# A six-layer model on one core: causal mask by matmuls, totals inverted in a compact form, matmuls in TensorE's gaps

## The reference

```python
x = x + 0.5 * L0_ffn(ln(x))     # gated feed-forward, hidden size 512, ternary weights
x = x + L0_attn(ln(x))          # linear attention: theta, phi, g
x = x + 0.5 * L0_ffn(ln(x))
x = x + 0.5 * L1_ffn(ln(x))     # 8 low-rank experts, 2 chosen for each sequence
x = x + L1_attn(ln(x))          # causal softmax attention, 16 heads of 8, rotary positions
x = x + 0.5 * L1_ffn(ln(x))
```

## Time and profile before

| | |
|---|---|
| median of three runs | 767.94 us (765.27 to 769.16) |
| profiled execution | 768.91 us, of which span 765.8 us |
| TensorE busy | 656.6 us (86%), granted clock 0.931 in the mean |
| VectorE, ScalarE, GpSimd busy | 524.9, 504.1, 311.3 us |
| GpSimd selects (L1264) | 128, 79.8 us |
| 128x256 reciprocals (L1091) | 15, 26.2 us |
| DMA | 18.2% of 16 engines' span |

### The profile page before, as it was taken

The page is one execution under the profiler, slowest core; times in us unless marked ns, Lnnn a source line. Parts: engine busy times, 40 slices in busy tenths (PEclk is TensorE's granted clock), DMA queues, the critical chain, the costliest instruction groups (busy, mean ns, idle before and its releaser), DMA issues.

```text
span 765.8 us, 13407 instructions
## 1 busy us (share of the span) xinstructions
PE 656.6 (86%) x4878; PEld 468.1 (61%) x4878; DVE 524.9 (69%) x1306; ACT 504.1 (66%) x830; POOL 311.3 (41%) x433
## 2 busy tenths in 40 slices
PE   2889989999999998999999897877778778888673
PEld 1667766787777787777787774544445445545442
DVE  3745465677657755677678659988799867879342
ACT  2867677977689858878778952365545666655541
POOL 2200121143423130225345467566747665446432
PEclk9989999999999999999999998699889998989785
DMA  9100000000110000000111123134444353431111
GB/s 296 42 1 1 0 1 1 0 1 2 42 41 1 0 1 1 1 0 1 42 42 42 42 114 113 51 118 144 136 138 136 132 192 118 144 126 58 56 57 29
DMA packets 47083, 47.21 MB, mean 62 GB/s; under 512 B 3240, under 2 KB 41128, under 8 KB 46760
## 3 DMA queue, kind: packets, MB, share of 16 engines
q1 hardware_dynamic: 47016, 46.33, 18.2%
HBM read 23.51 MB, written 22.54 MB: 60 GB/s over the span
## 4 chain that ended last, share of the span: by engine, by line
PE 50%; DVE 17%; ACT 12%; DMA 8%; issue 6%; SPq 4%; POOL 2%; POOLq 0%; DVEq 0%; ACTq 0%
PE PSA L769 15%; PE PSA L773 14%; DMA LC<-do 5%; DVE MX L1070 5%; ACT PSA L1122 3%; PE PSA L935 2%; SPq L1316 2%; PE PSA L786 2%; DVE LC L1091 2%; DVE G L993 2%; DMA QS<-dq 2%; PE PSA L882 2%; ACT G L1118 2%; PE PSA L875 2%; ACT ah L1129 1%
## 5 line engine op out<-in xcount | busy, mean ns | idle before, releaser
L1216 POOL TENSOR_TENSOR RS<-VE,MHALF 128x4 f32<-128x4 f32 x48 | 49.3, 1027 | 228.6 <-DVE VE L975 228.4
L769 PE MATMUL PSA<-ah,WH 128*128 128x512 f32 x320 | 131.8, 412 | 9.0 <-DVE al L998 4.8
L1070 DVE TENSOR_REDUCE MX<-PSA 128x6 f32<-128x768 f32 x128 | 117.2, 945 | 16.3 <-PE PSA L904 16.3
L773 PE MATMUL PSA<-al,WH 128*128 128x512 f32 x320 | 125.9, 393 | 0.0
L1122 ACT ACTIVATE PSA<-PSA,SC 128x512 f32<-128x512 f32 x128 | 84.7, 661 | 55.4 <-PE PSA L773 54.8
L1198 ACT ACTIVATE PB<-PSA 128x768 f32<-128x768 f32 x128 | 99.0, 818 | 16.1 <-PE PSA L922 15.9
L769 PE MATMUL PSA<-bh,WH 128*128 128x512 f32 x256 | 104.7, 409 | 4.8 <-DVE al L998 1.7
L773 PE MATMUL PSA<-bl,WH 128*128 128x512 f32 x256 | 100.2, 392 | 0.0
L1264 POOL TENSOR_SCALAR_AFFINE_SELECT PB<-PB 128x512 f32<-128x512 f32 x128 | 79.8, 635 | 45.2 <-ACT PB L1198 43.6
L998 DVE TENSOR_TENSOR al<-PSA,ah 128x512 fp32r<-128x512 f32 x64 | 44.2, 691 | 67.0 <-ACT ah L1129 67.0
L769 PEld LDWEIGHTS PSA<-ah,WH 128*128 128x128 f32 x320 | 60.5, 189 | 27.0 <-DVE al L998 7.1
(11 more groups left out here) (120 smaller groups left out, 1355.9 us busy)
## 6 DMA issues: line engine op xcount, KB each, us to landing
do<-OT SPq DMA_DIRECT2D x15, 512.0 KB, 4.7
KS<-dk SPq DMA_DIRECT2D x32, 192.0 KB
QS<-dq SPq DMA_DIRECT2D x32, 192.0 KB
dk<-CB SPq DMA_DIRECT2D x16, 192.0 KB, 2.3
dq<-CB SPq DMA_DIRECT2D x16, 192.0 KB, 2.5
X<-in_x SPq DMA_DIRECT2D x8, 256.0 KB, 6.9
dk<-CB SPq DMA_DIRECT2D x16, 128.0 KB, 1.9
dq<-CB SPq DMA_DIRECT2D x16, 128.0 KB, 1.9
```

The lines of the kernel that those rows point to most:

```text
L769: e.matmul(o, WH[:, col:col + 128], hi, start=first, stop=False)
L773: return e.matmul(o, WH[:, col:col + 128], low, start=False, stop=last)
L1070: e.tensor_reduce(MX[:, u % 2, :, :].rearrange("p t (l g) -> p l t g", l=2)[:, :, :, g], PSA[:, b:b + 2, 0:384].rearrange("p l (t k) -> p ...
L1216: e.tensor_tensor(RS[:, i, :], VE[:, i, :], MHALF[:, :], ALU.pow).then_inc(g_rs, 1)
```

## The change

1. `pass2`: `affine_select` on GpSimd goes. Four matmuls ahead of the scores add -1e30 where keys lie after the query, from the identity IM and a new constant ML (two more casts on GpSimd in `mark`, a masks input of 384 KB for 256). `weigh` waits for ScalarE's exp.
2. For units 0 to 13 the totals are inverted once for each head and query: `tot_in` loads one row of totals for each head as 128x32 (TOT), `inverse` inverts it on VectorE, `tot_out` writes it to DRAM, `vl_in` loads it to LC with a broadcast over the eight rows of a head. `norm_out` waits for the loads. Unit 14 keeps the load and reciprocal of before, the reciprocal placed up to 3 us earlier in the plan; unit 15 keeps `spread`. The layouts of DO, WO and SEL change to match.
3. `fill`: after `mark`, wherever the planned start of a TensorE step lies after the end of the one before, a step `keep` with up to 65% of the gap in 128x128 bf16 matmuls (identity times identity, 0.06 us each in the plan) goes in before it. It writes to the bank that is free first, which nobody reads.

```diff
-    "pass2": [("P", 0.18, 0.34), ("A", 0.69, 0.81), ("G", 0.59, 0.63)],
+    "pass2": [("P", 0.34, 0.5), ("A", 0.69, 0.81)],
+    "tot_in": [("S", 0.5, 0.5), ("D", 2.6)], "inverse": [("V", 0.28, 0.36)],
+    "tot_out": [("S", 0.5, 0.5), ("D", 2.6)], "vl_in": [("S", 1.12, 1.12), ("D", 3.7)], "recip": [("V", 1.66, 1.74)], "norm_out": [("G", 0.68, 0.72)],
+FILLED = 0.65
...
+            if eng == "P":
+                self.fill(s0)
+                self.idle_from = s0 + us
...
+    def fill(self, t):
+        free = {b: f for b, f in [*enumerate(self.bank), *self.sr.free.items()] if f}
+        if not free or not self.count.get("mark"):
+            return
+        b = min(free, key=lambda b: self.left(free[b]))
+        n = int((t - max(self.idle_from, self.left(free[b]) + 0.06) - 0.15) * FILLED / 0.06)
+        if n > 1:
...
+            self.steps.insert(-1, Step("keep", k, x=n, b=b, emptied=free[b]))
...
             yield from self.until(o.done - 0.5)
+            if u < NB - 2:
+                o = self.put("tot_in", u=u, src=o)
+                yield from self.until(o.done)
+                o = self.put("inverse", u=u, src=o)
+                yield from self.until(o.done - 0.2)
+                o = self.put("tot_out", u=u, src=o)
+                yield from self.until(o.done - 0.5)
             ld = self.put("vl_in", u=u, src=o, emptied=self.vcfree[u % 2])
             self.vcfree[u % 2] = None
-            yield from self.until(ld.done)
-            rc = self.put("recip", u=u, src=ld)
-            on = self.put("norm_out", u=u, src=rc)
+            yield from self.until(ld.done - 3.0 * (u == NB - 2))
+            if u == NB - 2:
+                ld = self.put("recip", u=u, src=ld)
+                yield from self.until(ld.done - 0.2)
+            on = self.put("norm_out", u=u, src=ld)
...
+                elif st.name == "keep":
+                    w.wait_ge(g_c, 4)
+                    emptied(w, st.emptied)
+                    for _ in range(st.x):
+                        e.matmul(PSA[:, b, 0:128], IDB[:, :], IDB[:, :], start=True, stop=True)
...
+                    for k in (1, 0):
+                        for h in range(2):
+                            e.matmul(PSA[:, b + h, 0:256].rearrange("p (t q) -> p t q", t=2)[:, :, 0:64 + 64 * k],
+                                     IM[64 * h:64 * h + 64, k, :], ML[64 * h:64 * h + 64, k, :, 0:64 + 64 * k],
+                                     start=(k == 1), stop=False, skip_group_check=True)
...
-                    w.wait_ge(g_sel, 8 * u + 2 * g + 2)
+                    w.wait_ge(a_prob, 8 * u + 2 * g + 2)
...
+                elif st.name == "inverse":
+                    w.wait_ge(s_tot[u % 2], 16 * (u // 2 + 1))
+                    e.reciprocal(TOT[:, u % 2, :], TOT[:, u % 2, :]).then_inc(v_inv, 1)
...
-                elif st.name == "pass2":
-                    w.wait_ge(a_prob, n + 1)
-                    e.affine_select(out=P, in_=P, compare_op=ALU.is_ge, fill=0.0, base=0,
-                                    pattern=[[0, 4], [1, 128]], channel_multiplier=-1).then_inc(g_sel, 1)
                 elif st.name == "norm_out":
-                    w.wait_ge(v_rc, st.src.n + 1)
+                    if st.src.name == "recip":
+                        w.wait_ge(v_rc, st.src.n + 1)
+                    else:
+                        w.wait_ge(s_vl[u % 2], 32 * (u // 2 + 1))
...
+                elif st.name == "tot_in":
+                    w.wait_ge(s_dv[u % 2], 16 * (u // 2 + 1))
+                    w.wait_ge(s_inv[u % 2], 16 * (u // 2))
+                    e.dma_start(TOT[:, u % 2, :], DO[u, 8].rearrange("v g (a b) -> (v g a) b", b=32)).then_inc(
+                        s_tot[u % 2], 16)
+                elif st.name == "tot_out":
+                    w.wait_ge(v_inv, st.src.n + 1)
+                    e.dma_start(DI[u].rearrange("v g (a b) -> (v g a) b", b=32), TOT[:, u % 2, :]).then_inc(
+                        s_inv[u % 2], 16)
...
+                        w.wait_ge(s_inv[u % 2], 16 * (u // 2 + 1))
+                        totals = DI[u:u + 1].rearrange("o v g t -> o (v g) t").to_broadcast([8, 16, S])
```

More of the change, by code:

```diff
@@ L141, in __init__ @@
         self.table = self.pe = ""
+        self.idle_from = 0.0
         self.lay()
@@ L175, in put @@
         return st
+    def fill(self, t):
[5 more added lines that the diff above has]
+        if n > 1:
+            self.note("P", max(self.idle_from, self.left(free[b]) + 0.06), max(self.idle_from, self.left(free[b]) + 0.06) + 0.06 * n, "keep")
+            k = self.count.get("keep", 0)
+            self.count["keep"] = k + 1
+            self.steps.insert(-1, Step("keep", k, x=n, b=b, emptied=free[b]))
     def note(self, eng, a, z, name):
@@ L569, in build @@
         MK = sb("MK", [128, 2, 2, 128], BF16)
+        ML = sb("ML", [128, 2, 2, 128], BF16)
         SC = sb("SC", [128, 17])
@@ L605, in build @@
         BT = XT[:, 1, :].rearrange("p (k d) -> p k d", k=4)
-        MASKS = XP[:, 0, :].rearrange("p (k d) -> p k d", k=4)
+        MASKS = XP[:, :, :].rearrange("p a (k d) -> p (a k) d", k=4)[:, 0:6, :]
         RA = sb("RA", [128, 2, TC])
@@ L643, in build @@
         LC = sb("LC", [128, 2, S])
+        TOT = sb("TOT", [128, 2, 32])
         SEL = sb("SEL", [128, 8, 128])
@@ L647, in build @@
         DKK = nc.dram_tensor("dk", [NB, 6, 2, 8, 8, S], BF16)
-        DO = nc.dram_tensor("do", [NB, 4, 32, 4, S], F32)
+        DO = nc.dram_tensor("do", [NB, 32, 4, 4, S], F32)
+        DI = nc.dram_tensor("di", [NB, 4, 4, S], F32)
         s_w = [sem(f"s_w{i}") for i in range(5)]
@@ L656, in build @@
         s_vl = [sem(f"s_vl{u}") for u in range(2)]
+        s_tot = [sem(f"s_tot{u}") for u in range(2)]
+        s_inv = [sem(f"s_inv{u}") for u in range(2)]
+        v_inv = sem("v_inv")
         s_out, s_sel, p_spread, v_on = sem("s_out"), sem("s_sel"), sem("p_spread"), sem("v_on")
@@ L674, in build @@
         v_turn, v_mx, v_peak, v_mt, v_rc = (sem(n) for n in ("v_turn", "v_mx", "v_peak", "v_mt", "v_rc"))
-        g_c, g_rs, g_xn, g_ones, g_wb, g_turn, g_rest, g_sel, g_on = (
-            sem(n) for n in ("g_c", "g_rs", "g_xn", "g_ones", "g_wb", "g_turn", "g_rest", "g_sel", "g_on"))
+        g_c, g_rs, g_xn, g_ones, g_wb, g_turn, g_rest, g_on = (
+            sem(n) for n in ("g_c", "g_rs", "g_xn", "g_ones", "g_wb", "g_turn", "g_rest", "g_on"))
         xin = I["x"].rearrange("b (c p) d -> p (b c) d", p=128)
@@ L918, in tensor @@
                     emptied(w, st.emptied)
-                    for k in range(2):
+                    for k in (1, 0):
[3 more added lines that the diff above has]
+                                     start=(k == 1), stop=False, skip_group_check=True)
+                    for k in (1, 0):
                         for h in range(2):
@@ L923, in tensor @@
                                          K[64 * h:64 * h + 50, g, 128 * k:128 * k + 128],
-                                         Q[64 * h:64 * h + 50, g, 128 * k:256], start=(k == 0), stop=True,
+                                         Q[64 * h:64 * h + 50, g, 128 * k:256], start=False, stop=(k == 0),
                                          skip_group_check=True)
@@ L1229, in gpsimd @@
                     for k in range(2):
-                        t = e.tensor_copy(MK[:, :, k, :], MASKS[:, 2:4, :])
+                        e.tensor_copy(MK[:, :, k, :], MASKS[:, 2:4, :])
+                        t = e.tensor_copy(ML[:, :, k, :], MASKS[:, 4:6, :])
                     t.then_inc(g_c, 1)
@@ L1260, in gpsimd @@
                     e.tensor_tensor(CB[:, g, 2, :], RA[:, 0, :], CB[:, g, 1, :], ALU.subtract).then_inc(g_rest, 1)
-                elif st.name == "pass2":
-                    P = PB[:, n % 4, 0:2, :, :].rearrange("p t l q -> p (t l) q")
-                    w.wait_ge(a_prob, n + 1)
-                    e.affine_select(out=P, in_=P, compare_op=ALU.is_ge, fill=0.0, base=0,
-                                    pattern=[[0, 4], [1, 128]], channel_multiplier=-1).then_inc(g_sel, 1)
                 elif st.name == "norm_out":
-                    w.wait_ge(v_rc, st.src.n + 1)
+                    if st.src.name == "recip":
+                        w.wait_ge(v_rc, st.src.n + 1)
+                    else:
+                        w.wait_ge(s_vl[u % 2], 32 * (u // 2 + 1))
                     e.tensor_tensor(VC[:, u % 2, :], VC[:, u % 2, :], LC[:, u % 2, :], ALU.mult).then_inc(g_on, 1)
@@ L1324, in sync @@
                     w.wait_ge(a_ot, st.src.n + 1)
-                    e.dma_start(DO[u].rearrange("v r g t -> (v r) g t"), OT[u % 2][:, :, :]).then_inc(s_dv[u % 2], 16)
+                    e.dma_start(DO[u].rearrange("r v g t -> v r (g t)"), OT[u % 2][:, :, :]).then_inc(s_dv[u % 2], 16)
+                elif st.name == "tot_in":
[7 more added lines that the diff above has]
+                        s_inv[u % 2], 16)
                 elif st.name == "vl_in":
@@ L1329, in sync @@
                         w.wait_ge(p_proj, s.n + 1)
```

(21 more changed lines are left out.)

## The result

The changed kernel takes 786.7 us (783.78 to 788.59) against 768.55 us (765.27 to 769.71) for the one before: 1.024 times as long, 95% interval 1.019 to 1.029. I had forecast 750 us, in 732 to 767. It is slower, and lies outside the range.

A forecast was written before the change was run, and what follows sets the result against it. The prediction took VectorE to bound the attention stage, TensorE close behind, and TensorE the feed-forward stage. Gains of 30.8 us less costs of 12.7 gave -18.1, 750.8 us, stated as 750, range 732 to 767.

The forecast's parts named there:

- Two more DMAs per unit: SyncE's queue: tot_in and tot_out, each waited for, cost 3 us (bounds 0 and 26), plus 1 us for unit 13.
- Rival 3: SyncE becomes late: half of each unit's extra 5.3 us exposed, 26 us instead of 3, 773 us; chance 0.13.
- the terms for the totals: Compact totals: -14 us reciprocals, +3 two small DMAs, +1 unit 13 finishing later, -3 unit 14 placed earlier.
- Reciprocals: VectorE, attention stage: 128x32 at 0.30 us for 1.746; 17.3 us leave, four fifths arrive, -14 us (bounds 9 and 17.3).
- rival 1: All of VectorE's relief arrives, 17.3 us for 14 its first term; no mask cost before 709 us; 735 us; chance 0.22.
- Mask by matmul: Attention stage and end: selects gone -1.5 us, VectorE released -3; TensorE's extra matmuls cost +3 before 709 us, +2.7 after.
- unit 14's order: At the end: unit 14's reciprocal placed 3 us earlier in the plan, -3 us; unit 13 finishing later, +1 us.
- The release of VectorE by the missing select: VectorE's peak operations in the attention stage, no longer held up by GpSimd's selects: -3 us (bounds 0 and 7).
- Fills: TensorE's gaps: higher clock gives -4, -2.8 and -2.5 us; late fills cost 1 (feed-forward) and 2 (attention).
- Rival 2: The clock stays as it is: fills miss gaps and come late, 9.3 us of gain go, 3 added; 762 us; chance 0.15.
- Order at the end: Unit 14's reciprocal placed 3 us earlier, so the chain at the end follows the last unit: -3 us.

The follow-up runs named there:

- e5: The kernel before with only the layout of DO changed (store, loads, WO and SEL to match): 1.009 of before.
- e6: The whole changed kernel with its store ot_out issued as four DMAs of 32 rows: 750.94 us, 0.981 of before.
- e3: The changed kernel without fills and compact totals, so mask by matmuls alone in the new layout of DO: 1.024 of before.
- e7: Mask by matmuls alone, with the old layout of DO and unit 14's reciprocal early: 0.986 of before.
- e10: The changed kernel with the store in four, compact totals alone (mask on GpSimd, no fills): 0.980 of before.
- e9: The changed kernel with the store in four and no fills (mask by matmuls and compact totals): 0.984 of before.
- e8: Fills alone, with the old layout of DO, mask on GpSimd, totals as before, unit 14's reciprocal early: 0.997 of before.
- e11: The changed kernel with the store in four, fills planned at 0.10 us each, only 16 of 32 rows stored: 749.69 us, 0.976 of before.

## Why the prediction was wrong, step by step

- **The step that failed** is in the part "Two more DMAs per unit". It costs the hops tot_in and tot_out and takes the store ot_out as it was. The diff moves DO, and the prediction has no term for it: the sum put the new layouts of DO, WO and SEL at nothing, without a reason. The Trainium skill has the rule on the very page (DMA: Bandwidth & Descriptors) that I cited for a fixed cost. Measured: the store takes 8.3 to 8.9 us for 1.4; the layout alone costs 7 us net of its faster loads (e5), and the store's pattern some 35 us in the changed kernel (against e6). The store stands in front of the next unit's loads on a few engines, and the compact totals have three more transfers behind it in series; the mask's plan, too, lost 3.8% by it (e3 against e7). Why a plan with the select on GpSimd and old totals loses only 0.9% isn't settled: SyncE there waits 55 us for the store instead of 15, and most of it is hidden. The faster loads don't explain it, since e3 has them too and loses 3.8%.
- **Rival 3** is nearest in number (773) and right that SyncE is late, for a wrong reason and only partly in the right place: on the chain the load of QS fell from 6.5% to 2.3%, and the totals' hops and MT came in. With the store repaired, the hops cost no more than was priced: e10 is faster than before by 15.7 us, where the terms for the totals were -14 + 3 + 1 - 3 = -13, though the 15.7 us have the faster load of VC in them. VectorE waits 3.1 us for TOT in e10; in e6, behind the mask's matmuls, 10.9 us.
- **Reciprocals: the price is right, how much of it arrives isn't shown.** 0.35 us for 0.30, VectorE's stage 20 us lighter (193 us in e10 for 213 in the earlier trace rows). The stage became 22.6 us shorter in e10, as if all of it arrived, not four fifths (the first term of rival 1). But e10 also has the new layout, with its load of VC over more engines than before. The run that would part the two, the old totals with the new layout and the store in four, was not made, so the 0.980 of e10 is the worth of both.
- **Mask by matmul: its gain mis-sized, its cost in the wrong place.** Alone it was to give -1.5 - 3 + 3 + 2.7 = +1.2 us, with unit 14's order -2; e7 gives -11 us (-14 to -8). Its span is 10.0 us shorter, 3.3 of them up to the last maximum and 6.7 after it. Behind compact totals the attention stage is its whole 19 us longer and the span 8 us (e9 against e10), where I put 3 + 2.7 as the cost and as much as the gain. The sizes fit one reading, that a TensorE microsecond is cheap only while VectorE is the bound; it was not tried by itself. The release of VectorE by the missing select was mis-sized: the operation with two inputs gave 15 x (0.435 - 0.248) = 2.8 us, but all three operations of `peak` fell, from 6.0 + 5.8 + 6.5 to 3 x 3.7 us, which is 7.2 us, about my upper bound, where I took 3. The prediction misread the operation before it, too: L1080 has one tensor as input, and L1078 before that has two.
- **Fills: right in mechanism, the value too high.** The granted clock rose, over the run from 0.938 (e9) to 0.979 (e6), after the last maximum from 0.77 to 1.00. But e8 gives 0.997, 2 us (0 to 5), where I had 9.3 - 3, and e6 against e9 is not separable. The plan's 0.06 us a fill holds at the full clock. Where the clock is still at half, a fill lasts 0.10 us, and real work waits for it, as at 779 us above; how much of the difference that is, no run shows. In e11, with 328 fills for 613, nothing is seen to be gained. The feed-forward stage neither gained nor lost. Rival 2 lies 12 us over the forecast: it has the fills cost 6 us where the forecast has them gain 6. The measured gain of 2 us is between the two, and the rival's reason, that the clock stays as it is, is wrong.
- **Order at the end: not tested alone.** It is in every run but e5, and so in the 0.986 of e7 and the 0.997 of e8.

The forecast sum, 750.8 us, met e6 at 750.9 us, with errors of both signs in its terms: a coincidence in part, and the forecast was for another kernel.

## What to carry to other kernels

Read every access pattern that a diff touches, also where the bytes stay the same, and ask what its slowest dimension is on either side: 128 rows of 4 KB left in 1.4 us over 16 engines and in 8.6 us over 4. When a DMA's latency shows on the chain, look at who is in front of it on the DMA engines before the hops themselves are blamed; a mean DMA share of a third hides four engines that are full. A new layout can help the loads and hurt the store at once, so follow each of its transfers by itself. When a matmul's price is read from a trace, read the granted clock of that stretch with it. And terms don't add when the bound moves: price a cost against the engine that bounds after the gain, not before it.

## What the runs showed of the hardware that I had not expected

- Splitting one store in four made the changed kernel some 35 us faster, in two 75 us slower, with the same bytes at the same addresses.
- Reciprocals: 1746 ns on 128x256 and 349 ns on 128x32, so by a line through the two, an estimate, 6.2 ns an element and 150 ns beside it.
- Back-to-back 128x128 bf16 matmuls, each with its own weights, came at 0.06 us each at a granted clock of 1.00 (48 in 2.84 us) and at 0.10 us each at 0.50 (44 in 4.51 us).
- The loads of VC and LC, 128 rows of 1 KB each, took 3.2 to 4.0 us for the pair as 4 by 32 rows and 1.1 to 1.3 us as 128.
- Without the selects on GpSimd, all three short VectorE operations of `peak` fell, from 385 to 435 ns to 244 to 248 ns in the mean, the one with a single input tensor (L1080) as well.
